# Two attention layers over 2,048 nodes on one core: nine XOR mask tiles instead of six, one compare moved from VectorE to ScalarE, and the part sums placed later

## The chip, the cores and the metric

The kernel runs on one NeuronCore of a Trainium2 chip. It is one program with no partner. The metric is the device time of one execution in microseconds; lower is better. PE is the matmul engine (PEld its weight loads), DVE the vector engine, ACT the scalar engine, POOL and SP the two engines that mostly start transfers.

## The reference

`x` is 2048x512, `adj` 2048x2048 with entries 0 and 1. The program applies a first attention layer (8 heads, over a list of related pairs), a residual, a layer norm, and then the second one, which alone is touched here:

```python
seq = (x @ W_seq).reshape(N, H, DH)                # N = 2048, H = 16 heads, DH = 32
score1 = jnp.einsum('nhd,d->hn', seq, a1)
score2 = jnp.einsum('nhd,d->hn', seq, a2)
scores = score1[:, :, None] + score2[:, None, :]
scores = jax.nn.leaky_relu(scores, negative_slope=ALPHA)
scores = scores + (1.0 - adj)[None, :, :] * MASK_VAL
attn = jax.nn.softmax(scores, axis=-1)
hidden = jnp.einsum('hij,jhd->ihd', attn, seq).reshape(N, D_IN)
```

The kernel forms no matrix of scores. The exponential of a leaky relu of a sum is one of two products of a factor of the target and a factor of the source, and which of them holds depends on the sign of score1 + score2 alone. So for each head it needs a 0/1 mask of neighbours with positive sign ("near") and one of neighbours with negative sign, and multiplies both with values that carry the two source factors.

## The kernel before, in words

The program runs in five blocks with a barrier between them. Block 4 (`stage4`) is the second attention: 16 heads `n`, and in each 16 source tiles `j` of 128 nodes, in an order that is written out in the code and fully unrolled. Each engine runs its own list in order, and semaphores tie the lists.

For one source tile `j` of head `n`:

- A **sign** makes `masks[:, j, :]` (128x2048, fp8) from the sum of scores: on ACT (line 990), or on DVE (`vector_sign`, line 1024) for the tiles in `VECTOR_SIGN`.
- DVE's **mask** (line 1032) ANDs it with the adjacency tile `adjT`.
- For the tiles in `FAR`, DVE's **far** (line 1038) XORs the mask with `nadjT` into `fars`, which is the mask of negative signs. `far(n, j)` stands behind `mask(n, j + 1)`.
- PE's **step** takes the tile in two halves of 1,024 targets, 8 pairs of matmuls in each. A tile in `FAR` costs two matmuls of 99 columns to a pair (lines 1132 and 1133, "far pair"). Any other costs one of 198 columns and one of 99 (lines 1135 and 1136, "near pair"): the negative mask is then the adjacency minus the near mask, by sign and accumulation. Half 1 lags half 0 by `LAG = 4` tiles, so that a head ends with four steps of half 1. `psum_done[0]` and `psum_done[1]` are set by the last step of each half. A head's first step waits for `bank_free[0]`.

Once for each head, among the masks, stand:

- `values(n + 1)` on DVE (lines 1008 and 1012) makes `tmp`, the values of the next head. **part 0** on ACT (line 979) copies it to bf16; `take_off 0` on DVE (line 1019) subtracts that and signals `rest`; **part 1** on ACT copies what is left, and waits for `rest`; `take_off 1` on DVE subtracts again and signals `split`, for which PE's next head waits. Part 0 also waits for `psum_done[1]` of the head before the present one.
- `sum_parts(n - 1, half)` on DVE (line 1047) waits for `psum_done[half]`, adds up the PSUM parts and frees the banks. Then come `scale` (1055), `join` (1063), `invert` (1067) and `norm` (1071).

```python
def part(m, b, p):
    act.wait_ge(*((value, 2 * (m + 1)) if p == 0 else (rest, m + 1)))
    if p == 0 and m >= 2:
        act.wait_ge(psum_done[1], m - 1)
    act.activation(V[:, b, :, p, :], tmp[:, :, :], ACT.Copy).then_inc(hi_out if p == 0 else mid_out, 1)
```

Of the kernel before, what the change touches and what calls it, by code (L numbers as in the profile page):

```python
# [48 lines left out]
HB = 16  # L49
# [879 lines left out]

HALF = N // 2  # L930
HT = HALF // P
VECTOR_SIGN = (3, 8, 13)
FAR = (1, 4, 6, 9, 11, 14)
NS = NT - len(VECTOR_SIGN)
LAG = 4
CZ = 2 * DZ
# [2 lines left out]
def stage4(nc, c, io, t, s, ps):  # L939
# [7 lines left out]
    masks = sb("masks", [P, NT, N], F8)  # L947
    fars = sb("fars", [P, len(FAR), N], F8)
    s1b = [sb(f"s1b{i}", [P, N]) for i in range(2)]
# [11 lines left out]
    with nc.Block() as block:  # L961
        @block.sync
        def _(sp):
            def load(n, b):
                sp.dma_start(s1b[b][:, :], t["s1_rows"][n:n + 1, :].to_broadcast([P, N])).then_inc(s1_in[b], 16)
            load(0, 0)
            load(1, 1)
            for n in range(HB - 2):
                sp.wait_ge(mask_ready, NT * (n + 1))
                load(n + 2, n % 2)  # L970

        @block.scalar
        def _(act):
# [7 lines that stand above are left out]
            def head(n, b):  # L981
                act.wait_ge(s1_in[b], 8 * (n - b) + 16)
                for j in range(NT):
                    if j not in VECTOR_SIGN:

                        if j < NT - 1:
                            act.wait_ge(mask_used, (NT - 1) * n + j + 1)
                        elif n > 0:
                            act.wait_ge(psum_done[1], n)
                        act.activation(masks[:, j, :], s1b[b][:, :], ACT.Relu, bias=t["s2"][:, n, 0, j:j + 1], scale=BIG,  # L990
                                       saturate=False).then_inc(signs, 1)
                    if j in (5, 11) and n < HB - 1:
                        part(n + 1, 1 - b, 0 if j == 5 else 1)
            part(0, 0, 0)
            part(0, 0, 1)
            for n in range(HB):
                head(n, n % 2)

        @block.vector
        def _(dve):  # L1000
# [3 lines left out]
            def values(m):  # L1004

                if m > 0:
                    dve.wait_ge(split, m)
                dve.tensor_tensor(tmp[:, :, :].rearrange("p j (k z) -> p j k z", k=2)[:, :, :, 0:DH],
                                  seq[:, :, None, m * DH:(m + 1) * DH].to_broadcast([P, NT, 2, DH]),
                                  t["e"][:, :, :, m:m + 1].rearrange("p k j o -> p j k o").to_broadcast([P, NT, 2, DH]),  # L1010
                                  ALU.mult).then_inc(value, 1)
                dve.tensor_copy(tmp[:, :, :].rearrange("p j (k z) -> p j k z", k=2)[:, :, :, DH:DZ],
                                t["e"][:, :, :, m:m + 1].rearrange("p k j o -> p j k o")).then_inc(value, 1)

            def take_off(m, b, p):

                dve.wait_ge(hi_out if p == 0 else mid_out, m + 1)
                out = tmp[:, :, :] if p == 0 else V[:, b, :, 2, :]
                dve.tensor_tensor(out, tmp[:, :, :], V[:, b, :, p, :], ALU.subtract).then_inc(rest if p == 0 else split, 1)

            def vector_sign(n, b, j):
                dve.wait_ge(mask_used, (NT - 1) * n + j + 1)
                dve.wait_ge(s1_in[b], 8 * (n - b) + 16)
                dve.tensor_scalar(masks[:, j, :], s1b[b][:, :], t["s2"][:, n, 1, j:j + 1], NEAR, ALU.is_gt, ALU.mult,
                                  saturate=False).then_inc(vector_signs, 1)

            def mask(n, j):
                if j in VECTOR_SIGN:
                    dve.wait_ge(vector_signs, len(VECTOR_SIGN) * n + VECTOR_SIGN.index(j) + 1)
                else:  # L1030
                    dve.wait_ge(signs, NS * n + sum(x not in VECTOR_SIGN for x in range(j)) + 1)
                dve.tensor_tensor(masks[:, j, :].bitcast(U32), masks[:, j, :].bitcast(U32), adjT[:, j, :].bitcast(U32),  # L1032
                                  ALU.bitwise_and).then_inc(mask_ready, 1)

            def far(n, j):

                dve.wait_ge(mask_ready, NT * n + j + 1)
                dve.tensor_tensor(fars[:, FAR.index(j), :].bitcast(U32), nadjT[:, j, :].bitcast(U32),  # L1038
                                  masks[:, j, :].bitcast(U32), ALU.bitwise_xor).then_inc(far_ready, 1)

            def sum_parts(n, half):

                dve.wait_ge(psum_done[half], n + 1)
                if n > 0:
                    dve.wait_ge(scaled, n)
                    dve.wait_ge(joined, n)
                dve.reduce_sum(sums[:, half * HT:(half + 1) * HT, :, :].rearrange("p t k d -> p t (k d)"),
                               ps[:, 4 * half:4 * half + 4, :].rearrange("p b (u c) -> p (b u) c", u=2)[:, :, 0:3 * CZ]
                               .rearrange("p t (s c) -> p t c s", s=3), AX.X).then_inc(summed, 1)
                dve.wait_ge(summed, 2 * n + half + 1)  # L1050
                dve.sem_inc(bank_free[half], 1)

            def scale(n):
                dve.wait_ge(summed, 2 * n + 2)
                dve.tensor_tensor(sums[:, :, :, :], sums[:, :, :, :],
                                  t["w"][:, n, :, :, None].to_broadcast([P, NT, 2, DZ]), ALU.mult).then_inc(scaled, 1)

            def join(n):

                dve.wait_ge(scaled, n + 1)  # L1060
                if n > 0:
                    dve.wait_ge(normed, n)
                dve.tensor_tensor(hid[:, :, :], sums[:, :, 0, :], sums[:, :, 1, :], ALU.subtract).then_inc(joined, 1)

            def invert(n):
                dve.wait_ge(joined, n + 1)
                dve.reciprocal(rz[:, :], hid[:, :, DH]).then_inc(inverse, 1)

            def norm(n):
                dve.wait_ge(inverse, n + 1)  # L1070
                dve.tensor_tensor(seq[:, :, n * DH:(n + 1) * DH], hid[:, :, 0:DH],
                                  rz[:, :, None].to_broadcast([P, NT, DH]), ALU.mult).then_inc(normed, 1)

            def head(n, b):
                for j in range(NT):
                    if j + 1 in VECTOR_SIGN:
                        vector_sign(n, b, j + 1)
                    mask(n, j)
                    if j - 1 in FAR:
                        far(n, j - 1)  # L1080
                    if n > 0:
                        if j == 2:
                            sum_parts(n - 1, 0)
                        if j == 5:
                            sum_parts(n - 1, 1)
                        if j == 7:
                            scale(n - 1)
                        if j == 8:
                            join(n - 1)
                        if j == 9:  # L1090
                            invert(n - 1)
                        if j == 11:
                            norm(n - 1)
                    if n < HB - 1:
                        if j == 1:
                            values(n + 1)
                        if j == 6:
                            take_off(n + 1, 1 - b, 0)
                        if j == 12:
                            take_off(n + 1, 1 - b, 1)  # L1100
            values(0)
            take_off(0, 0, 0)
# [1 line left out]
            for n in range(HB):  # L1104
                head(n, n % 2)
# [9 lines left out]
        def _(pe):  # L1115
            pe.sem_inc(mask_used, NT - 1)

            def step(n, b, half, j):
# [4 lines left out]
                pe.wait_ge(mask_ready, NT * n + j + 1)  # L1123
                if j in FAR:
                    pe.wait_ge(far_ready, len(FAR) * n + FAR.index(j) + 1)
                for i in range(HT):
# [3 lines left out]
                    then = dict(start=False, stop=(j == NT - 1), skip_group_check=True)  # L1130
                    if j in FAR:
                        pe.matmul(out[:, :, 0:DZ], masks[:, j, cols], V[:, b, j, :, 0:DZ], **first)  # L1132
# [215 lines left out]
```

## Time and profile before

| | |
|---|---|
| median of 3 runs | 1426.04 us (1421.89 to 1428.71) |
| profiled execution | 1427.51 us, its span 1426.0 us |
| PE, DVE, ACT, POOL busy over the span | 87%, 75%, 54%, 21% |
| block 4: first sign to last matmul of the last head | 853.14 us to about 1342.5 us |

A row of the timeline gives the start, the length and the engine, line and operation of an instruction, or of several of one kind in a row. The length of one instruction holds a tail in which the next has already begun: what an instruction costs in a full row is the distance from its start to the start of the next.

### The profile page before, as it was taken

How to read it: one execution, taken by the hardware profiler on the slowest of the kernel's cores; microseconds unless marked ns; L12 is line 12 of the kernel's file. 1: busy time of each engine (PE TensorE's matmuls, PEld its weight loads, DVE VectorE, ACT ScalarE, POOL GpSimd, SP SyncE). 2: the span in 40 equal slices, each digit the busy share in tenths (PEclk: the TensorE clock that was granted, in tenths of full speed). 3: DMA queues.
4: the chain of work that ended last, by engine and by line, in shares of the span. 5: the costliest groups of instructions: out<-in, count | busy, mean ns of one | idle time of the engine just before them, and what ended most of it. 6: DMA issues, size and time to landing. Idle time of an engine off the chain costs nothing. (4 is left out here: it accounts for less than half of the span.)

```text
span 1426.0 us, 26813 instructions
## 1 busy us (share of the span) xinstructions
PE 1245.6 (87%) x11026; PEld 839.5 (59%) x11026; DVE 1063.6 (75%) x1411; ACT 764.6 (54%) x763; POOL 306.5 (21%) x247
## 2 busy tenths in 40 slices
PE   4885066999999999989978948999999999999797
PEld 2442022344444444444434528999999999999743
DVE  4576047999999999986214978899898899898455
ACT  2221054454545444442213449899998999989122
POOL 2588643222223233300003630000000000000011
PEclk9998588999999999999998978999999999999999
DMA  6744132122222222212118640000110000100141
GB/s 260 217 116 134 17 70 52 48 68 68 68 68 68 68 48 54 51 27 59 45 41 219 105 105 31 32 31 32 53 40 32 31 32 32 61 32 2 52 148 74
DMA packets 81268, 99.61 MB, mean 70 GB/s; under 512 B 44401, under 2 KB 60032, under 8 KB 79120
## 3 DMA queue, kind: packets, MB, share of 16 engines
q1 hardware_dynamic: 71024, 69.91, 15.6%
q0 software_dynamic: 10144, 28.24, 9.5%
q8 instruction: 78, 1.28, 0.4%
q14 instruction: 22, 0.18, 0.0%
HBM read 88.20 MB, written 20.33 MB: 76 GB/s over the span
## 5 line engine op out<-in xcount | busy, mean ns | idle before, releaser
L990 ACT ACTIVATE s_masks<-s_s1b,s 128x2048 fp8e4<-128x2048 f32 x208 | 396.7, 1987 | 0.0
L1135 PE MATMUL psum<-s_V,s_masks 128*128 128x198 bf16 x2560 | 352.9, 249 | 15.1 <-DVE s_masks L1032 15.1
L1136 PE MATMUL psum<-s_V,nadjT 128*128 128x99 bf16 x2560 | 347.6, 209 | 0.0
L579 ACT ACTIVATE s_exp<-psum,s_negm 128x1536 f32<-128x1536 f32 x96 | 148.0, 1542 | 232.3 <-DVE s_W L648 184.9
L1135 PEld LDWEIGHTS psum<-s_V,s_masks 128*128 128x128 fp8e4 x2560 | 250.2, 98 | 15.7 <-issue 15.4
L1136 PEld LDWEIGHTS psum<-s_V,nadjT 128*128 128x128 fp8e4 x2560 | 250.5, 98 | 0.0
L518 PE MATMUL psum<-h,s_WT 128*128 128x512 f32 x512 | 240.6, 598 | 0.0
L640 DVE TENSOR_SCALAR_CACHE_REDUCE s_junkv<-psum 128x1536 bf16<-128x1536 f32 x96 | 168.5, 1755 | 57.2 <-PE psum L538 55.3
L1032 DVE TENSOR_TENSOR s_masks<-s_masks,adjT 128x512 uint32<-128x512 uint32 x256 | 169.4, 681 | 49.5 <-ACT s_masks L990 47.0
L535 PE MATMUL psum<-f_keys,f_q 128*128 128x512 bf16 x288 | 112.2, 390 | 88.0 <-PEq L221 58.7
L648 DVE SCALAR_TENSOR_TENSOR s_W<-s_exp,s_r,s_W 128x1536 f32<-128x1536 f32 x84 | 179.3, 2135 | 0.2
L1132 PE MATMUL psum<-s_V,s_masks 128*128 128x99 bf16 x1536 | 158.7, 209 | 4.1 <-DVE s_fars L1038 3.4
L1133 PE MATMUL psum<-s_V,s_fars 128*128 128x99 bf16 x1536 | 158.6, 209 | 0.0
L1132 PEld LDWEIGHTS psum<-s_V,s_masks 128*128 128x128 fp8e4 x1536 | 142.3, 98 | 6.1 <-DVE s_masks L1032 3.6
L1133 PEld LDWEIGHTS psum<-s_V,s_fars 128*128 128x128 fp8e4 x1536 | 142.6, 97 | 0.0
L1282 POOL DMA_DIRECT2D out<-s_x x16 | 8.9, 553 | 569.3 <-DVE s_x L1205 569.3
L518 PEld LDWEIGHTS psum<-h,s_WT 128*128 128x128 f32 x512 | 89.5, 192 | 69.7 <-issue 69.7
L535 PEld LDWEIGHTS psum<-f_keys,f_q 128*128 128x128 bf16 x288 | 28.7, 100 | 150.8 <-issue 76.1
L537 PE MATMUL psum<-f_keys,f_q 128*128 128x512 bf16 x288 | 112.2, 390 | 0.0
L536 PE MATMUL psum<-f_keys,f_q 128*128 128x512 bf16 x288 | 112.0, 389 | 0.0
L538 PE MATMUL psum<-f_low,identb 128*128 128x512 bf16 x288 | 111.9, 388 | 0.0
L284 POOL DMA_INDIRECT rel_planes<-s_ones,s_flat x80 | 101.3, 1266 | 49.0 <-issue 33.8
(141 smaller groups left out, 1620.8 us busy)
## 6 DMA issues: line engine op xcount, KB each, us to landing
s_s1b<-s_rows SPq DMA_DIRECT2D x16, 1024.0 KB, 4.7
f_q<-q_parts SPq DMA_DIRECT2D x72, 128.0 KB, 3.2
f_adj<-in_adj POOLq DMA_DIRECT2D x16, 512.0 KB, 5.2
s_adj<-in_adj POOLq DMA_DIRECT2D x16, 512.0 KB, 5.2
rel_planes<-s_zero POOLq DMA_DIRECT2D x3, 2304.0 KB, 19.2
f_rel<-rel_planes SPq DMA_DIRECT2D x36, 192.0 KB, 3.1
f_keys<-s_parts SPq DMA_DIRECT2D x48, 128.0 KB, 2.8
s_x<-x SPq DMA_DIRECT2D x6, 1024.0 KB, 12.3
```

Of the source, the lines that this page charges most:

```text
L518: last = pe.matmul(ps[:, 7, :], WT[m % 2][:, b, :], h[:, 2 * m + b, :], start=(m == 0 and b == 0), stop=(m == HA - 1 and b == 1))
L535: pe.matmul(out, qs[q][:, 0, hd, :], f.k1[:, hd, cols], start=True, stop=False)
L537: pe.matmul(out, qs[q][:, 2, hd, :], f.k2[:, hd, cols], start=False, stop=False)
L579: act.activation(ex[:, hd, :], ps[:, 3 * (hd % 2):3 * (hd % 2) + 3, :].rearrange("p c j -> p (c j)"), ACT.Exp, bias=negm[:, b, hd:hd + 1], ...
L640: dve.tensor_scalar(junkv[:, :], ps[:, 3 * (hd % 2):3 * (hd % 2) + 3, :].rearrange("p c j -> p (c j)"), -1.0, -DIAG, ALU.mult, ALU.min, ac ...
L648: dve.scalar_tensor_tensor(w[:, 0:NE], ex[:, hd, :], r8[:, hd:hd + 1], w[:, 0:NE], ALU.mult, ALU.add).then_inc(added, 1)
L990: act.activation(masks[:, j, :], s1b[b][:, :], ACT.Relu, bias=t["s2"][:, n, 0, j:j + 1], scale=BIG, saturate=False).then_inc(signs, 1)
L1032: dve.tensor_tensor(masks[:, j, :].bitcast(U32), masks[:, j, :].bitcast(U32), adjT[:, j, :].bitcast(U32), ALU.bitwise_and).then_inc(mask_r ...
L1132: pe.matmul(out[:, :, 0:DZ], masks[:, j, cols], V[:, b, j, :, 0:DZ], **first)
L1133: last = pe.matmul(out[:, :, DZ:CZ], fars[:, FAR.index(j), cols], V[:, b, j, :, DZ:CZ], **then)
L1135: pe.matmul(out, masks[:, j, cols], V[:, b, j, :, :], **first)
L1136: last = pe.matmul(out[:, :, DZ:CZ], nadjT[:, j, cols], V[:, b, j, :, DZ:CZ], **then)
```

## The change

Nine tiles instead of six are in `FAR`. `VECTOR_SIGN` has two tiles instead of three, so that ACT makes 14 signs in a head and DVE two. ACT's part 0 stands behind the sign of tile 7 (was 5), part 1 behind that of 12 (was 11). On DVE `values` stands after mask 3 (was 1), the two part sums after masks 4 and 6 (were 2 and 5), `norm` after mask 10 (was 11), `take_off 0` after mask 11 (was 6) and `take_off 1` after mask 14 (was 12).

```diff
-VECTOR_SIGN = (3, 8, 13)
-FAR = (1, 4, 6, 9, 11, 14)
+VECTOR_SIGN = (2, 8)
+FAR = (0, 1, 3, 4, 6, 9, 10, 12, 14)
...
-                    if j in (5, 11) and n < HB - 1:
-                        part(n + 1, 1 - b, 0 if j == 5 else 1)
+                    if j in (7, 12) and n < HB - 1:
+                        part(n + 1, 1 - b, 0 if j == 7 else 1)
...
-                        if j == 2:
+                        if j == 4:
                             sum_parts(n - 1, 0)
-                        if j == 5:
+                        if j == 6:
                             sum_parts(n - 1, 1)
...
-                        if j == 11:
+                        if j == 10:
                             norm(n - 1)
                     if n < HB - 1:
-                        if j == 1:
+                        if j == 3:
                             values(n + 1)
-                        if j == 6:
+                        if j == 11:
                             take_off(n + 1, 1 - b, 0)
-                        if j == 12:
+                        if j == 14:
                             take_off(n + 1, 1 - b, 1)
```

DVE's list before, in head 1, from the second part sum (after mask 5) over `take_off 0` (line 1019, after mask 6) to `join`:

```order
L1047 TENSOR_REDUCE s_sums<-psum 128x528
L1032 TENSOR_TENSOR s_masks<-s_masks,adjT 128x512
L1019 TENSOR_TENSOR s_tmp<-s_tmp,s_V 128x1056
L1024 TENSOR_SCALAR s_masks<-s_s1b,s 128x2048
L1032 TENSOR_TENSOR s_masks<-s_masks,adjT 128x512
L1038 TENSOR_TENSOR s_fars<-nadjT,s_masks 128x512
L1055 TENSOR_TENSOR s_sums<-s_sums,w 128x1056
L1032 TENSOR_TENSOR s_masks<-s_masks,adjT 128x512
L1063 TENSOR_TENSOR s_hid<-s_sums 128x528
```

DVE's list of the change, in head 1, from `invert` (after mask 9) to `take_off 0` (after mask 11) and on to `take_off 1` (after mask 14):

```order
L1067 RECIPROCAL s_rz<-s_hid 128x16
L1032 TENSOR_TENSOR s_masks<-s_masks,adjT 128x512
L1038 TENSOR_TENSOR s_fars<-nadjT,s_masks 128x512
L1071 TENSOR_TENSOR seq<-s_hid,s_rz 128x16x32
L1032 TENSOR_TENSOR s_masks<-s_masks,adjT 128x512
L1038 TENSOR_TENSOR s_fars<-nadjT,s_masks 128x512
L1019 TENSOR_TENSOR s_tmp<-s_tmp,s_V 128x1056
L1032 TENSOR_TENSOR s_masks<-s_masks,adjT 128x512 x2
L1038 TENSOR_TENSOR s_fars<-nadjT,s_masks 128x512
L1032 TENSOR_TENSOR s_masks<-s_masks,adjT 128x512
L1019 TENSOR_TENSOR s_V<-s_tmp,s_V 128x16x66
```

`take_off 0` has moved from before `scale` to behind the whole of `scale`, `join`, `invert` and `norm`, and three masks and two XORs stand between it and `invert`.

ACT's list before, from the first part 0 (line 979) on; the signs between part 0 and part 1 are five, and from part 1 to the next part 0 eight:

```order
L979 ACTIVATE s_V<-s_tmp 128x16x66
L990 ACTIVATE s_masks<-s_s1b,s 128x2048 x5
L979 ACTIVATE s_V<-s_tmp 128x16x66
L990 ACTIVATE s_masks<-s_s1b,s 128x2048 x8
L979 ACTIVATE s_V<-s_tmp 128x16x66
```

The same place of the change:

```order
L979 ACTIVATE s_V<-s_tmp 128x16x66
L990 ACTIVATE s_masks<-s_s1b,s 128x2048 x4
L979 ACTIVATE s_V<-s_tmp 128x16x66
L990 ACTIVATE s_masks<-s_s1b,s 128x2048 x10
L979 ACTIVATE s_V<-s_tmp 128x16x66
```

Four signs now stand between part 0 and part 1 and ten behind part 1; the ten are those of tiles 13, 14 and 15 of the head and of 0, 1, 3, 4, 5, 6 and 7 of the next.

## Rows read from the trace of the kernel before

**Rows 1.** Busy times by window, one head long: PE, PEld, DVE, ACT, POOL, clock, DMA

```profile
core 0: us, PE busy (x) PEld busy (x) DVE busy (x) ACT busy (x) POOL busy (x), PEclk, DMA share, GB/s
930.00:960.00 30.00, 29.96 (x516) 29.83 (x513) 26.85 (x36) 26.66 (x16) 0.00 (x0) 1.00 0.11 37
```

**Rows 2.** Waits from 1005.68 to 1035.68 us: us in total, times, longest

```profile
DVE s_masks L1032 <- ACT s_masks L990: 2.8, 3, 1.3
```

**Rows 3.** Timeline of PE: two near pairs, 31 pairs apart

```profile
1000.19 0.25 PE L1135 MATMUL psum<-s_V,s_masks 128*128 128x198 bf16 x1
...
1004.25 0.25 PE L1135 MATMUL psum<-s_V,s_masks 128*128 128x198 bf16 x1
```

**Rows 4.** Timeline of ACT over one head; in brackets the idle time before

```profile
1012.83 1.09 ACT L979 ACTIVATE s_V<-s_tmp 128x1056 bf16<-128x1056 f32 x1 [3.34 <-PE psum L1136]
...
1023.28 1.07 ACT L979 ACTIVATE s_V<-s_tmp 128x1056 bf16<-128x1056 f32 x1
...
1042.83 1.08 ACT L979 ACTIVATE s_V<-s_tmp 128x1056 bf16<-128x1056 f32 x1 [3.33 <-PE psum L1136]
```

**Rows 5.** Timeline of DVE in the same head

```profile
1004.45 1.22 DVE L1008 TENSOR_TENSOR s_tmp<-seq,e 128x1024 f32<-128x1024 f32 x1
...
1005.68 1.28 DVE L1024 TENSOR_SCALAR s_masks<-s_s1b,s 128x2048 fp8e4<-128x2048 f32 x1
...
1008.15 1.81 DVE L1047 TENSOR_REDUCE s_sums<-psum 128x528 f32<-128x1584 f32 x1
1010.11 1.89 DVE L1032 TENSOR_TENSOR s_masks<-s_masks,adjT 128x512 uint32<-128x512 uint32 x3
...
1016.44 1.25 DVE L1019 TENSOR_TENSOR s_tmp<-s_tmp,s_V 128x1056 f32<-128x1056 f32 x1
1017.61 1.28 DVE L1024 TENSOR_SCALAR s_masks<-s_s1b,s 128x2048 fp8e4<-128x2048 f32 x1
1018.81 0.68 DVE L1032 TENSOR_TENSOR s_masks<-s_masks,adjT 128x512 uint32<-128x512 uint32 x1
1019.41 0.68 DVE L1038 TENSOR_TENSOR s_fars<-nadjT,s_masks 128x512 uint32<-128x512 uint32 x1
1020.01 1.25 DVE L1055 TENSOR_TENSOR s_sums<-s_sums,w 128x1056 f32<-128x1056 f32 x1
1021.18 0.68 DVE L1032 TENSOR_TENSOR s_masks<-s_masks,adjT 128x512 uint32<-128x512 uint32 x1
1021.78 0.70 DVE L1063 TENSOR_TENSOR s_hid<-s_sums 128x528 f32<-128x528 f32 x1
1022.40 0.68 DVE L1032 TENSOR_TENSOR s_masks<-s_masks,adjT 128x512 uint32<-128x512 uint32 x1
1023.00 0.24 DVE L1067 RECIPROCAL s_rz<-s_hid 128x16 f32<-128x16 f32 x1
1023.17 0.62 DVE L1032 TENSOR_TENSOR s_masks<-s_masks,adjT 128x512 uint32<-128x512 uint32 x1
...
1024.91 0.68 DVE L1071 TENSOR_TENSOR seq<-s_hid,s_rz 128x512 f32<-128x512 f32 x1
1025.51 1.28 DVE L1024 TENSOR_SCALAR s_masks<-s_s1b,s 128x2048 fp8e4<-128x2048 f32 x1
```

**Rows 6.** Timeline of ACT at the first signs of the block

```profile
852.15 1.08 ACT L979 ACTIVATE s_V<-s_tmp 128x1056 bf16<-128x1056 f32 x1 [1.32 <-DVE s_tmp L1019]
853.14 9.56 ACT L990 ACTIVATE s_masks<-s_s1b,s 128x2048 fp8e4<-128x2048 f32 x5
```

**Rows 7.** Timeline of DVE: first mask, head 0's second part sum, the last part sum

```profile
855.15 0.69 DVE L1032 TENSOR_TENSOR s_masks<-s_masks,adjT 128x512 uint32<-128x512 uint32 x1 [0.64 <-ACT s_masks L990]
...
892.75 1.81 DVE L1047 TENSOR_REDUCE s_sums<-psum 128x528 f32<-128x1584 f32 x1 [0.16 <-PE psum L1136]
...
1342.55 1.81 DVE L1047 TENSOR_REDUCE s_sums<-psum 128x528 f32<-128x1584 f32 x1 [2.81 <-PE psum L1136]
```

**Rows 8.** Busy times by window around the end of the last head (columns as in rows 1)

```profile
1342.00:1346.00 4.00, 0.51 (x8) 0.32 (x6) 3.27 (x3) 0.00 (x0) 0.00 (x0) 1.00 0.00 0
...
1354.00:1358.00 4.00, 3.92 (x5) 1.83 (x6) 0.00 (x0) 0.00 (x0) 0.00 (x0) 0.51 0.90 246
```

## The prediction, on record before the changed kernel ran

> **What bounds the kernel now.** I looked first at the busy shares of the whole span, where PE leads, and then only at block 4, since no other block is touched. The windows of one head's length show PE busy for 29.96 of 30.00 us, DVE for 26.85, ACT for 26.66 [rows 1]. The reader is to see that PE has no gap, while the two others have about 3 us each. The list of waits of such a head says where these are: DVE waits 2.8 us for signs of ACT [rows 2], and ACT waits 3.34 us for PE, before part 0, which wants the head before to be finished [rows 4]. That is slack: PE holds ACT back. Part 0 begins every 30.00 us (1012.83, 1042.83) [rows 4]. So before, a head costs what its matmuls cost. About 0.5% of this kernel, 7 us, is what its measurement can tell from no change.
>
> **PE's share of the change.** Two near pairs 31 pairs apart start 4.06 us apart, 0.131 us for a pair [rows 3]. A head has 160 near and 96 far pairs; 160 x 0.131 = 20.96, and the 8.99 left of about 29.95 make 0.0936 us for a far pair. Three more far tiles turn 3 x 16 = 48 pairs: 48 x 0.0374 = 1.80 us less. PE then needs 28.15 us a head. If PE still set the pace that would be 16 x 1.80 = 29 us.
>
> **ACT's share.** From part 0 at 1012.83 to part 1 at 1023.28 there are 10.45 us: 0.99 for the part (852.15 to 853.14 [rows 6]), five signs of 1.892 [rows 4]. A head with 14 signs and two parts costs 14 x 1.892 + 1.98 = 28.47 us without a wait, already more than PE's 28.15. So at best the change gives 30.00 - 28.47 = 1.5 us a head.
>
> **DVE's share.** By distance between starts [rows 5]: a mask 0.60 (1021.18 to 1021.78), an XOR 0.60 (1019.41 to 1020.01), a sign 1.20 (1017.61 to 1018.81), `values` 1.23, a part sum with its release of the banks 1.96, `scale` 1.17, `join` 0.62, `invert` 0.17 (the mask behind it is 0.06 shorter than others, 0.62 against 0.68 in length), `norm` 0.60, `take_off` 1.17, or 1.25 until its signal. Three XORs more and a sign less are 1.80 - 1.20 = +0.60. A head's work becomes 9.54 + 5.40 + 2.40 + 1.23 + 3.92 + 1.17 + 0.62 + 0.17 + 0.60 + 2.34 = 27.4 us. No engine alone is over 28.5.
>
> **Where the waits go.** The moved pieces close a loop that was slack before. Part 1 on ACT waits for `take_off 0`. Behind part 1 in ACT's list stand the signs of tiles 13, 14, 15 and of the next head's 0 and 1. DVE's mask 1 waits for that last one, and then goes in order through all up to the next `take_off 0`, for which the next part 1 waits. Before, `take_off 0` stood after mask 6 and part 1 five signs after part 0, so part 1 found it done: no idle time stands before the row at 1023.28 [rows 4]. Now it stands after mask 11 and XOR 10, behind both part sums, `scale`, `join`, `invert` and `norm`. One turn of the loop:
>
> - ACT: part 1 to the first sign 0.99; five signs, the last to its end, 4 x 1.892 + 1.99 = 9.56. Sign to mask is 0.02 to 0.03 (853.14 + 1.99 to 855.15 [rows 6, 7]), and I take the same from `take_off 0` to part 1. Together 10.60.
> - DVE from mask 1: eleven masks 6.54, XORs of tiles 0, 1, 3, 4, 6, 9, 10 4.20, `values` 1.23, two part sums 3.92, the sign of tile 8 1.20, `scale` 1.17, `join` 0.62, `invert` 0.17, `norm` 0.60, `take_off 0` to its signal 1.25. Together 20.90.
>
> The turn is 31.50 us, one head. To enter DVE at a neighbour of mask 1 gives less: at mask 0 it is 1.89 less on ACT and 0.60 + 1.20 more on DVE (31.4), at mask 3 it is 1.89 more and 2.40 less (31.0). So the pace is 31.5: ACT idles 31.5 - 28.5 = 3.0 before part 1, and DVE then starves, since the signs that it wants next are queued behind part 1: with part 1 at time 0, DVE has mask 12 done at 0.5 and waits until sign 13 ends at 3.0; again about 0.7 before masks 14 and 0 each, some 4 us in a head.
>
> I checked what else is late in that clock. XOR 14 ends at 8.0, so PE ends half 0 near 10.6 and the head near 15.25 (0.75, 0.75 and 1.05 for steps 14, 10 and 15; then 1.05, 0.75, 1.05, 0.75, 1.05). DVE reaches the first part sum at 16.0 and the second at 19.8, ACT part 0 at 19.9: none waits for PE. The banks come free at 17.9, so **PE idles some 2.6 us at each head's start**, and 0.7 before step 14. From 17.9 its 28.15 us would end the head at 46.05, 5.2 before the second sum of the next head wants it (51.3).
>
> **The sum.** The first sign starts at 853.14 [rows 6], and nothing ahead of it changes. In head 0 ACT is the pace: part 0 after seven signs at 866.39, four more signs start at 867.38, and tile 11's ends at 873.15; mask 11, XOR 10 and `take_off 0` make it 875.62, part 1 at 875.65. (Head 0's PE end is wanted by the sum at 895.4; before it was there at 892.75 [rows 7], with more matmul work.) Fourteen turns of 31.50 bring the last part 1 to 1316.65. In the last head there is no `values`; mask 4 waits for its sign (14.33), and the banks are free at about 17.45. PE's 28.15 us then end at 1316.65 + 45.6 = 1362.25, against 1342.5 before (the last part sum starts at 1342.55 [rows 7]). That is +19.7 us; block 5 follows as it did. The profiled execution was 1427.51 us, so 1447.2 on its scale; it lay 1.5 above the median of the runs shown, so **1446** for the median. An error of 0.2 us in a turn is 2.8 in the sum; with 0.3 the forecast's own range is 1441 to 1451.
>
> **A rule weighed.** Part 0 idles ACT for 3.34 us [rows 4] though the slot for the sign behind it had been free for some eight half steps of PE: the signs did not pass the waiting part. The Trainium skill, in TensorE: Matmul & The Clock Gate, section Architectural detail, says that the scalar and vector engines have strict first-in first-out queues and that PE alone pulls something ahead, its weight loads. By that rule, with which the trace agrees, part 1 blocks the signs and the turn is 31.5 us; without it ACT would be at 28.5.
>
> **Rivals.**
>
> 1. *ACT alone sets the pace, faster.* The three engines' own sums, 28.15, 28.47 and 27.4, speak for it. If `take_off 0` reached part 1 in time, or a wait of 0.5, a head would take 28.5 to 29.0: 15 heads x 1.0 to 1.5 less gives 1404 to 1411. It decides if DVE's run from mask 1 to the signal is under 28.47 - 10.60 = 17.9 us instead of 20.9. The rows leave no 3 us there. Chance 0.06.
> 2. *About as before.* A turn between 29.5 and 30.4 would do it; it needs 1.1 us or more out of the loop, say starts on DVE closer than 0.60 in a full run. Time 1419 to 1433. Chance 0.05.
> 3. *The clock falls in PE's new gaps, slower still.* PE was idle for about 3.5 us in a window that granted full speed (1342 to 1346), and later ran 3.92 of 4 us at 0.51, the 1.2 GHz level, when it began again after a longer idle time [rows 8]. Such a 4 us costs PE 2 us, and it has 5.2 to spare in a turn, so one dip a head only shows in the last head (+2, 1448). Three or four such stretches cost 6 to 8 us, 0.8 to 2.8 over what is spare; in 14 turns that is 11 to 39 us, 1457 to 1485. The Trainium skill, same page, Part 1: The HAM clock gate, says that idleness brings the clock down to half; by that rule each new gap could cost a dip. The row bears it out only for the longer idle time: 3.5 us of idleness still had full speed, and the new gaps are 2.6. Chance of more than a hidden dip 0.06.
> 4. *The loop as forecast:* chance 0.83, 1441 to 1451.
>
> **How the numbers follow.** Most likely 1446. Range 1438 to 1453: the forecast's own, widened for single waits on semaphores that a full list may show and for the spread of runs (1421.89 to 1428.71). Faster by over 0.5% 0.06, within it 0.05, slower by over 0.5% 0.89.
>
> **What would show it.** Right: ACT's part (line 979) waiting for DVE's `s_tmp` about 3 us, 15 times; DVE's masks waiting for ACT's signs about 4 us a head; PE waiting for the part sum (line 1047) about 2.6 us at each head's start; part 1 coming every 31.5 us; PE busy about 28.2 of 31.5. Wrong: ACT without a gap over two heads (rival 1), PE without one (rival 2), or a granted clock under 1.00 in the middle of block 4 (rival 3).

## The result and the profile after

The changed kernel takes 1448.34 us (median of 6 runs, 1441.08 to 1453.62) against 1424.57 us before (median of 6, 1420.37 to 1428.71). The ratio is 1.0159, with a 95% interval of 1.0122 to 1.0196: slower, and 2.3 us over the forecast of 1446. The profiled execution took 1453.62 us with a span of 1451.7.

The windows of one turn of ACT, 31.60 us long, show where the profile changed (PE, PEld, DVE, ACT, POOL, clock, DMA), against [rows 1]:

```profile
core 0: us, PE busy (x) PEld busy (x) DVE busy (x) ACT busy (x) POOL busy (x), PEclk, DMA share, GB/s
1030.00:1061.60 31.60, 28.39 (x516) 27.93 (x513) 27.56 (x38) 28.55 (x17) 0.00 (x0) 1.00 0.10 35
```

PE, DVE and ACT now each have 3 to 4 us of idle time in a head. None of them is the bound by itself, as the forecast loop between engines has it. The list of waits over thirteen heads (912 to 1322 us; us in total, times, longest) names its links:

```profile
DVE s_masks L1032 <- ACT s_masks L990: 47.3, 39, 2.4
ACT s_V L979 <- DVE s_tmp L1019: 39.5, 13, 3.0
PEld psum L1132 <- issue: 31.8, 19, 2.6
PE psum L1132 <- issue: 28.5, 13, 2.5
```

ACT waits for `take_off 0` 13 times for 3.0 us, and DVE three times a head for ACT's signs, 3.6 us together. PE is idle 13 times before a head's first far pair. No releaser is given there; I take it to be the bank release behind the first part sum, an instruction that the profile does not count as work: one such sum runs from 1021.42 to 1023.22 us and PE starts at 1023.38, and where the wait is shorter the profile names that release (experiment 4). The timeline of ACT shows it in place, where [rows 4] had no idle time before part 1:

```profile
1005.39 1.09 ACT L979 ACTIVATE s_V<-s_tmp 128x1056 bf16<-128x1056 f32 x1 [3.05 <-DVE s_tmp L1019]
1006.38 19.02 ACT L990 ACTIVATE s_masks<-s_s1b,s 128x2048 fp8e4<-128x2048 f32 x10
1025.31 1.07 ACT L979 ACTIVATE s_V<-s_tmp 128x1056 bf16<-128x1056 f32 x1
1026.28 7.67 ACT L990 ACTIVATE s_masks<-s_s1b,s 128x2048 fp8e4<-128x2048 f32 x4
1036.99 1.09 ACT L979 ACTIVATE s_V<-s_tmp 128x1056 bf16<-128x1056 f32 x1 [3.05 <-DVE s_tmp L1019]
```

Part 0 at 1025.31 waits for nothing, where before it waited 3.34 us for PE. DVE's timeline in the same turn:

```profile
1005.27 0.68 DVE L1032 TENSOR_TENSOR s_masks<-s_masks,adjT 128x512 uint32<-128x512 uint32 x1
1008.40 0.69 DVE L1032 TENSOR_TENSOR s_masks<-s_masks,adjT 128x512 uint32<-128x512 uint32 x1 [2.44 <-ACT s_masks L990]
...
1010.29 0.69 DVE L1032 TENSOR_TENSOR s_masks<-s_masks,adjT 128x512 uint32<-128x512 uint32 x1 [0.60 <-ACT s_masks L990]
...
1014.08 0.69 DVE L1032 TENSOR_TENSOR s_masks<-s_masks,adjT 128x512 uint32<-128x512 uint32 x1 [0.60 <-ACT s_masks L990]
1014.68 1.28 DVE L1024 TENSOR_SCALAR s_masks<-s_s1b,s 128x2048 fp8e4<-128x2048 f32 x1
1015.97 0.69 DVE L1032 TENSOR_TENSOR s_masks<-s_masks,adjT 128x512 uint32<-128x512 uint32 x1
...
1025.18 1.80 DVE L1047 TENSOR_REDUCE s_sums<-psum 128x528 f32<-128x1584 f32 x1
1027.20 1.29 DVE L1024 TENSOR_SCALAR s_masks<-s_s1b,s 128x2048 fp8e4<-128x2048 f32 x1 [0.22 <-DVE s_sums L1047]
...
1035.71 1.25 DVE L1019 TENSOR_TENSOR s_tmp<-s_tmp,s_V 128x1056 f32<-128x1056 f32 x1
```

One turn can be read off: part 1 at 1005.39, first sign behind it 1006.38, mask 1 at 1015.97 (10.58 us, forecast 10.60 with the step to part 1), `take_off 0` until 1035.71 + 1.25 = 1036.96 (20.99, forecast 20.90), next part 1 at 1036.99. From mask 1 on DVE has no wait but one of 0.22 behind the second part sum, before it could start tile 8's sign.

The stages ahead of block 4 differ by up to 12 us from one profiled execution to another: the first sign starts at 844 to 856 us in the eleven of this study. So block 4 is also measured by itself, from the first sign to the start of the last part sum. Before, it is 1342.55 - 853.14 = 489.4 us. In the changed kernel, by its timeline:

```profile
856.45 1.99 ACT L990 ACTIVATE s_masks<-s_s1b,s 128x2048 fp8e4<-128x2048 f32 x1
...
1367.05 1.81 DVE L1047 TENSOR_REDUCE s_sums<-psum 128x528 f32<-128x1584 f32 x1 [2.81 <-PE psum L1136]
```

That is 510.6 us, +21.2; the forecast sum was +19.7, and the medians differ by 23.8. The 2.6 us between 21.2 and 23.8 are not in block 4.

### The profile page after: what moved, and what is told of

It is laid out like the page before. It is cut to its first block and busy times, and to the rows that moved or that the text cites. A ratio compares the mean times of both kernels' runs of the same rounds, so it can differ in the third digit from the quotient of the medians.

```text
span 1451.7 us, 26895 instructions
## 1 busy us (share of the span) xinstructions
PE 1225.4 (84%) x10996; PEld 818.3 (56%) x11026; DVE 1072.4 (74%) x1443; ACT 795.0 (55%) x779; POOL 309.6 (21%) x247
## 5 line engine op out<-in xcount | busy, mean ns | idle before, releaser
L990 ACT ACTIVATE s_masks<-s_s1b,s 128x2048 fp8e4<-128x2048 f32 x224 | 427.0, 1987 | 0.0
L1132 PE MATMUL psum<-s_V,s_masks 128*128 128x99 bf16 x2304 | 238.4, 212 | 58.1 <-issue 33.0
L1135 PE MATMUL psum<-s_V,s_masks 128*128 128x198 bf16 x1792 | 259.7, 252 | 0.0
L1136 PE MATMUL psum<-s_V,nadjT 128*128 128x99 bf16 x1792 | 252.8, 210 | 0.0
L1133 PE MATMUL psum<-s_V,s_fars 128*128 128x99 bf16 x2304 | 238.5, 212 | 0.0
L1032 DVE TENSOR_TENSOR s_masks<-s_masks,adjT 128x512 uint32<-128x512 uint32 x256 | 174.8, 683 | 63.2 <-ACT s_masks L990 60.2
L1133 PEld LDWEIGHTS psum<-s_V,s_fars 128*128 128x128 fp8e4 x2304 | 217.1, 99 | 0.0
L1136 PEld LDWEIGHTS psum<-s_V,nadjT 128*128 128x128 fp8e4 x1792 | 177.0, 99 | 0.0
L536 PE MATMUL psum<-f_keys,f_q 128*128 128x512 bf16 x288 | 111.7, 388 | 68.9 <-PEq L221 62.1
L535 PE MATMUL psum<-f_keys,f_q 128*128 128x512 bf16 x260 | 101.3, 390 | 24.1 <-ACT s_exp L579 23.3
L537 PE MATMUL psum<-f_keys,f_q 128*128 128x512 bf16 x286 | 110.7, 387 | 0.0
```

The costliest lines, as they stand in the source:

```text
L535: pe.matmul(out, qs[q][:, 0, hd, :], f.k1[:, hd, cols], start=True, stop=False)
L536: pe.matmul(out, qs[q][:, 1, hd, :], f.k1[:, hd, cols], start=False, stop=False)
L1133: last = pe.matmul(out[:, :, DZ:CZ], fars[:, FAR.index(j), cols], V[:, b, j, :, DZ:CZ], **then)
L1135: pe.matmul(out, masks[:, j, cols], V[:, b, j, :, :], **first)
L1136: last = pe.matmul(out[:, :, DZ:CZ], nadjT[:, j, cols], V[:, b, j, :, DZ:CZ], **then)
```

## The experiments

Theory: the loop through part 1. Rivals tested: the late part sums (PE's new gap at each head's start) and the load of the tables (three more XORs, 14 signs). "Block 4" is the length defined above, of each run's profile; a ratio is to the kernel before on the same chip.

| kernel | ratio (95% interval) | block 4, us |
|---|---|---|
| changed | 1.0159 (1.0122 to 1.0196) | 510.6 |
| 1. `take_off 0` after mask 8 | 0.9801 (0.9758 to 0.9844) | 465.7 |
| 2. kernel before, `take_off 0` after mask 11 | 1.0092 (1.0057 to 1.0127) | 502.4 |
| 3. tables alone | 0.9929 (0.9893 to 0.9966) | 483.2 |
| 4. part sums back to 2 and 5 | 1.0128 (1.0082 to 1.0174) | 508.8 |
| 5. part 1 behind sign 14 | 0.9832 (0.9770 to 0.9893) | 465.8 |
| 6. as 1, part sums back | 0.9867 (0.9811 to 0.9922) | 466.3 |
| 7. `take_off 0` after mask 10 | 1.0035 (1.0005 to 1.0066) | 493.1 |
| 8. tables, both parts and `take_off 0` late | 0.9847 (0.9809 to 0.9884) | 465.7 |
| 9. as 6, part 0 behind sign 5 | 0.9925 (0.9896 to 0.9954) | 476.1 |

### 1. One line moved

```diff
-                        if j == 11:
+                        if j == 8:
                             take_off(n + 1, 1 - b, 0)
```

> The changed kernel with one line moved: take_off 0 stands after mask 8 again ahead of invert and norm, everything else as changed (nine XOR tiles, two DVE signs, part sums after masks 4 and 6). Theory (the loop through part 1): the DVE leg from mask 1 to the signal of take_off 0 loses masks 9, 10, 11, XORs 9 and 10, invert and norm, 21.0 - 3.7 = 17.3 us, so the turn is 10.6 + 17.3 = 27.9 us, under ACT's own 28.5; the idle time of ACT before part 1 goes from 3.0 to near 0 and a head takes 28.5 to 28.8 us. In all 15 x 3.0 = 45 us less than the changed kernel, about 0.984 of the kernel before. Rival (the late part sums, which free the banks late and leave PE a gap of 2.5 us in each head, cause the loss): they stay, so the time stays near 1.016. Rival (more DVE work, three XORs, causes it): stays near 1.016.

Measured: 0.9801, block 4 44.9 us shorter than in the changed kernel. The part sums and the XORs had stayed, so neither rival is enough to cause the loss. ACT's timeline has no idle time left in a turn of 28.46 us:

```profile
1008.47 1.07 ACT L979 ACTIVATE s_V<-s_tmp 128x1056 bf16<-128x1056 f32 x1
1009.45 19.03 ACT L990 ACTIVATE s_masks<-s_s1b,s 128x2048 fp8e4<-128x2048 f32 x10
1028.38 1.07 ACT L979 ACTIVATE s_V<-s_tmp 128x1056 bf16<-128x1056 f32 x1
1029.36 7.67 ACT L990 ACTIVATE s_masks<-s_s1b,s 128x2048 fp8e4<-128x2048 f32 x4
1036.93 1.07 ACT L979 ACTIVATE s_V<-s_tmp 128x1056 bf16<-128x1056 f32 x1
```

A window of one head shows how full all three engines are (columns as above):

```profile
1000.00:1028.46 28.46, 28.15 (x516) 27.93 (x514) 27.46 (x38) 28.46 (x18) 0.00 (x0) 1.00 0.11 39
```

PE 28.15, DVE 27.46, ACT 28.46: the three engine sums of the prediction (28.15, 27.4, 28.47). This version beats the kernel before by 2%, of which block 4, 23.7 us shorter, is 1.7%; there it is bound by ACT alone.

### 2. The suspected line alone, in the kernel before

```diff
-                        if j == 6:
+                        if j == 11:
                             take_off(n + 1, 1 - b, 0)
```

> The kernel before with take_off 0 alone moved from after mask 6 to after mask 11; six XOR tiles, three DVE signs, part sums after masks 2 and 5, part 1 after the sign of tile 11. Theory: the loop closes here too. ACT's leg with entry at mask 2 is 0.99 + 5 x 1.892 + 1.99 = 12.4 us, DVE's from mask 2 to the signal 18.5 us (six of its pieces once, ten masks, four XORs, two signs): a turn of 30.9 to 31.0 us against 30.0, some 13 us slower, 1.009. ACT shows a wait for line 1019 before each part 1. Rivals (part sums, or XORs and signs, cause the loss): no change, 1.000, and no such wait.

Measured: 1.0092, block 4 +13.0 us. The move slows the kernel without a single XOR more and with early part sums. ACT's timeline shows both its waits:

```profile
999.74 1.08 ACT L979 ACTIVATE s_V<-s_tmp 128x1056 bf16<-128x1056 f32 x1 [2.56 <-DVE s_tmp L1019]
1000.73 15.24 ACT L990 ACTIVATE s_masks<-s_s1b,s 128x2048 fp8e4<-128x2048 f32 x8
1017.55 1.09 ACT L979 ACTIVATE s_V<-s_tmp 128x1056 bf16<-128x1056 f32 x1 [1.58 <-PE psum L1136]
1018.55 9.56 ACT L990 ACTIVATE s_masks<-s_s1b,s 128x2048 fp8e4<-128x2048 f32 x5
1030.67 1.09 ACT L979 ACTIVATE s_V<-s_tmp 128x1056 bf16<-128x1056 f32 x1 [2.56 <-DVE s_tmp L1019]
```

DVE's timeline shows where the loop enters its list, and where it leaves it:

```profile
1010.33 0.69 DVE L1032 TENSOR_TENSOR s_masks<-s_masks,adjT 128x512 uint32<-128x512 uint32 x1 [1.20 <-ACT s_masks L990]
...
1029.38 1.25 DVE L1019 TENSOR_TENSOR s_tmp<-s_tmp,s_V 128x1056 f32<-128x1056 f32 x1
```

The turn is 30.93 us, expected 30.9 to 31.0, but the sum in the expectation was put together wrongly and came out right by luck. It entered DVE at mask 2 and counted the sign of tile 3, which stands ahead of mask 2. The entry is at mask 1, at 1010.33: ACT's leg is 10.59 us from part 1, DVE's 20.30 until `take_off 0` ends at 1030.63, and 0.04 lead to part 1. The wait for PE before part 0 is still there at 1.58 us, but it costs nothing: the loop leaves ACT's list at the sign of tile 1, ahead of part 0, and so does not pass through that wait.

### 3. The tables alone

```diff
-VECTOR_SIGN = (3, 8, 13)
-FAR = (1, 4, 6, 9, 11, 14)
+VECTOR_SIGN = (2, 8)
+FAR = (0, 1, 3, 4, 6, 9, 10, 12, 14)
```

> Of the change only the two tables: nine XOR tiles and two DVE signs; all pieces that stand once in a head stay where they were. Theory: no loop, ACT's 28.47 us sets the pace, 28.5 to 28.9 us a head, 18 to 24 us faster than before, 0.984 to 0.988. Rival (the load of the XORs on DVE or the 14 signs on ACT cause the loss): near 1.016. Rival (with DVE fuller, masks come late to PE): between 1.00 and 1.01.

Measured: 0.9929. Neither my 0.984 to 0.988 nor either rival: faster than before, but block 4 gained 6.2 us of the 23.7 that experiment 1 shows to be there. ACT still waits for PE before part 0, 0.5 and 1.9 us in turns, so that two heads take 59.53 us (980.93 to 1040.46):

```profile
980.93 1.08 ACT L979 ACTIVATE s_V<-s_tmp 128x1056 bf16<-128x1056 f32 x1 [1.91 <-PE psum L1136]
...
1009.99 1.09 ACT L979 ACTIVATE s_V<-s_tmp 128x1056 bf16<-128x1056 f32 x1 [0.49 <-PE psum L1136]
...
1040.46 1.08 ACT L979 ACTIVATE s_V<-s_tmp 128x1056 bf16<-128x1056 f32 x1 [1.91 <-PE psum L1136]
```

And PE waits for an XOR of DVE, up to 1.73 us:

```profile
1018.82 0.21 PE L1132 MATMUL psum<-s_V,s_masks 128*128 128x99 bf16 x1 [1.73 <-DVE s_fars L1038]
```

Each holds up the other, in a second loop, which takes two heads for a turn. More rows of ACT and of DVE show its links:

```profile
992.37 17.13 ACT L990 ACTIVATE s_masks<-s_s1b,s 128x2048 fp8e4<-128x2048 f32 x9
...
1003.85 0.69 DVE L1032 TENSOR_TENSOR s_masks<-s_masks,adjT 128x512 uint32<-128x512 uint32 x1
...
1017.99 0.68 DVE L1038 TENSOR_TENSOR s_fars<-nadjT,s_masks 128x512 uint32<-128x512 uint32 x1
```

Part 0 at 980.93 holds back the signs behind it, and the sixth of the nine from 992.37 on, tile 1's, ends as mask 1 starts at 1003.85: 22.92 us. DVE has no idle time from there to the XOR of tile 6 (1017.99), and PE starts that tile at 1018.82: 14.97. PE then has no gap up to the end of its head, for which part 0 at 1040.46 waits: 21.64. Together that is 59.53 us, where ACT's own work for two heads is 56.9. Experiments 6, 8 and 9 look for what opens this loop.

### 4. The part sums back

```diff
-                        if j == 4:
+                        if j == 2:
                             sum_parts(n - 1, 0)
-                        if j == 6:
+                        if j == 5:
                             sum_parts(n - 1, 1)
```

> The changed kernel with the two part sums back after masks 2 and 5. Theory: both still lie between mask 1 and take_off 0, so the turn stays at 31.5 to 31.6 us and the time at 1.016; PE's gap at each head's start shrinks or moves, and nothing is gained by it. Rival (the late sums cause the loss): the time falls to 0.984 to 1.00.

Measured: 1.0128, block 4 508.8 us against 510.6. ACT's wait stays at 2.98 us and its turn is 31.54 (1000.41 to 1031.95). The 0.06 a turn is the wait behind the second part sum, which a mask follows here. PE's idle time did not shrink, it moved (912 to 1290 us, twelve heads):

```profile
PE psum L1132 <- DVE s_fars L1038: 21.6, 48, 0.8
PE psum L1132 <- DVEq L1051: 9.6, 12, 0.8
```

A head starts 0.8 us late, by the bank release that is named here (line 1051), and the rest is in four short waits for XORs. So the long gap at the head's start was no cost of its own.

### 5. Part 1 behind sign 14

```diff
-                    if j in (7, 12) and n < HB - 1:
+                    if j in (7, 14) and n < HB - 1:
```

> The changed kernel with one number changed on ACT: part 1 stands behind the sign of tile 14 (changed kernel: 12); take_off 0 stays after mask 11 on DVE. Theory: the turn now has three signs behind part 1 (15, 0, 1) in place of five, 31.6 - 3.8 = 27.8 us, under ACT's 28.5, so ACT's idle time goes and a head takes 28.5 to 28.9 us: 0.980 to 0.985 of the kernel before. Should it be the place of take_off 0 on DVE alone that matters (the length of DVE's list ahead of it delays PE's masks), the time stays near 1.016.

Measured: 0.9832, block 4 465.8 us, no wait before either part. DVE's list is that of the changed kernel, instruction for instruction, `take_off 0` after mask 11 included. So its late place costs nothing in itself; only together with the signs queued behind part 1 does it close the loop.

### 6. Experiment 1 with early part sums

The edits of experiments 1 and 4 together.

> The changed kernel with take_off 0 after mask 8 and with the part sums back after masks 2 and 5. Tells what the late part sums are worth once the loop is open. Theory: the second sum has to wait for PE's end of a head, and XOR 6, for which PE waits, then stands behind it, so a head takes 28.9 to 29.5 us, 0.988 to 0.993 as with the tables alone. Rival (the later part 0, behind sign 7, is what the version with the tables alone lacked): 28.5 us a head, 0.980.

Measured: 0.9867, its interval overlaps that of experiment 1 (0.9801), and block 4 is 466.3 against 465.7 us. ACT runs without a gap. My theory for experiment 3, that the early second sum holds PE's masks up, falls: with early sums the loss is nil here. What experiment 3 lacked is among the other places: `values`, the two parts, `take_off 0` and `take_off 1`, `norm`. The difference of the two medians (1395.43 and 1406.31 us) does not come from block 4; in the profiled executions the first sign starts at 844.42 and 855.27 us. The granted clock from 150 to 300 us, far ahead of block 4, was 0.86 in the first and 0.81 in the second.

### 7. A dose

```diff
-                        if j == 11:
+                        if j == 10:
                             take_off(n + 1, 1 - b, 0)
```

> The changed kernel with take_off 0 after mask 10 (it was 11 in the changed kernel and 8 in an earlier run). A dose: DVE's leg loses mask 11 and XOR 10, 1.2 us, so the theory gives a turn of 31.60 - 1.20 = 30.40 us and 1.8 us of idle time before part 1; 15 x 1.2 = 18 us less than the changed kernel, 1.003 of the kernel before. If the loss were a threshold or had another cause, it would be 1.016 or 0.980.

Measured: 1.0035, as expected; ACT's timeline:

```profile
999.11 1.08 ACT L979 ACTIVATE s_V<-s_tmp 128x1056 bf16<-128x1056 f32 x1 [1.84 <-DVE s_tmp L1019]
...
1029.52 1.08 ACT L979 ACTIVATE s_V<-s_tmp 128x1056 bf16<-128x1056 f32 x1 [1.84 <-DVE s_tmp L1019]
```

The turn is 30.41 us (expected 30.40): one mask and one XOR less in DVE's leg, 1.2 us, are 1.19 us less a head. What stands in the leg comes through in full.

### 8 and 9. What the tables alone lacked

Experiment 8 takes the tables alone and moves the copies:

```diff
-                    if j in (5, 11) and n < HB - 1:
-                        part(n + 1, 1 - b, 0 if j == 5 else 1)
+                    if j in (7, 12) and n < HB - 1:
+                        part(n + 1, 1 - b, 0 if j == 7 else 1)
...
-                        if j == 6:
+                        if j == 8:
                             take_off(n + 1, 1 - b, 0)
```

> The version with the tables alone (0.993), with the copies moved besides: part 0 behind sign 7, part 1 behind sign 12, take_off 0 after mask 8. The part sums stay after masks 2 and 5, values after mask 1, norm after 11, take_off 1 after 12. With the tables alone ACT waited for PE before part 0, 0.5 and 1.9 us in turns, and PE for XORs. If part 0 stood too early there, ACT now runs without a gap and a head takes 28.5 us: block 4 from first sign to last part sum 466 us in place of 483, 0.982 to 0.987. If it was the early part sums or values, it stays at 483 us, 0.993.

Measured: 0.9847, block 4 465.7 us, no wait before a part. So `values`, `norm`, `take_off 1` and the sums could have stayed; the place of the two copies and of `take_off 0` was what experiment 3 lacked. Experiment 9 takes number 6 and moves part 0 alone back:

```diff
-                    if j in (7, 12) and n < HB - 1:
-                        part(n + 1, 1 - b, 0 if j == 7 else 1)
+                    if j in (5, 12) and n < HB - 1:
+                        part(n + 1, 1 - b, 0 if j == 5 else 1)
```

> The version with take_off 0 after mask 8 and the part sums after masks 2 and 5 (466 us for block 4), with one number changed: part 0 behind the sign of tile 5 in place of 7. If part 0 behind sign 5 makes ACT wait for PE's end of a head, the wait of 0.5 to 1.9 us before part 0 comes back and block 4 takes 475 to 485 us, 0.990 to 0.995. If the place of part 0 does not matter, it stays at 466 us.

Measured: 0.9925 and 476.1 us, in the range expected, but by another wait than I had named: not for PE, but for `values`:

```profile
1002.23 1.09 ACT L979 ACTIVATE s_V<-s_tmp 128x1056 bf16<-128x1056 f32 x1 [0.68 <-DVE s_tmp L1012]
...
1031.48 1.09 ACT L979 ACTIVATE s_V<-s_tmp 128x1056 bf16<-128x1056 f32 x1 [0.70 <-DVE s_tmp L1012]
```

DVE, in between:

```profile
1025.14 0.69 DVE L1032 TENSOR_TENSOR s_masks<-s_masks,adjT 128x512 uint32<-128x512 uint32 x1
...
1027.56 1.80 DVE L1047 TENSOR_REDUCE s_sums<-psum 128x528 f32<-128x1584 f32 x1
1029.51 0.69 DVE L1032 TENSOR_TENSOR s_masks<-s_masks,adjT 128x512 uint32<-128x512 uint32 x1
```

This is a third loop, of one head: from part 0 at 1002.23 over ACT's signs to mask 1 at 1025.14, then on DVE without idle time through the first part sum and `values` to part 0 at 1031.48, 29.25 us in all. The part sum makes up 1.95 of them. Without it 27.3 would be left, under ACT's 28.5, so by this estimate it takes the late `values` and the early sum together; that was not run.

A part 0 that stands early makes ACT wait, for whichever of its two conditions is late: PE's end of the head before where `values` stands after mask 1 (experiment 3), `values` where it stands after mask 3 and behind the first part sum (here). Whether part 0 alone, without part 1 and `take_off 0`, would have cured experiment 3 was not tried. An estimate says yes: two signs less between part 0 and sign 1 are 2 x 1.892 = 3.8 us less in its loop, 55.7 for two heads, under ACT's 56.9.

## Why the prediction was right, point by point

**The bound.** Right. The kernel before was PE's, and the three engine sums of the changed kernel were met to 0.1 us in experiment 1, where no loop disturbs them.

**The loop.** Right, and shown from three sides: with `take_off 0` earlier (1, 7), with fewer signs behind part 1 (5), and in the kernel before with only that line moved (2). The turn was 31.60 for a forecast 31.50. The 0.10 lies on DVE's leg, 20.99 in place of 20.90: 0.06 is the step from the second part sum to the sign of tile 8 (2.02 us, 1025.18 to 1027.20), which I priced like the step to a mask (1.96 [rows 5]). 14 turns of 0.10 are 1.4 of the 1.5 us by which block 4 passed the forecast; I had the mechanism and mis-sized this one term. Of the signs that I had listed, ACT's wait of 3.0 us came 14 times and not 15, since in head 0 it is 0.63, and DVE's waits are 3.6 us in a head in place of 4.

**The walk to the loop's first and last turn.** Part 1 of head 0 comes 22.53 us after the first sign (856.45 to 878.98, forecast 853.14 to 875.65, 22.51), and the last part sum starts 45.6 us after the last part 1 (1321.41 to 1367.05, forecast 45.6).

**The median.** Block 4 is where the sum was put to the test: 510.6 us against 489.4 + 19.7 = 509.1. That the median came within 2.3 us of 1446 is in part luck. The six runs spread over 12.5 us, the first sign of the profiled execution came 3.3 us later than before (856.45 against 853.14), and the sum had nothing for that.

**PE's gap at each head's start.** Right in kind: 28.5 us over 13 heads, 2.2 each against 2.6. The mean hides two sizes. In the twelve heads that start from 960 to 1308 us the gap is 2.47 us six times and 1.94 six times. It is 1.94 in a head that follows one with a fall of the clock (below), in which PE's work took longer. In the others PE also waits some 0.7 us, but for the XOR of tile 12 (1041.44, 4.45 us after part 1), where I had placed this wait before step 14. The gap's price of nothing was right (experiment 4).

**The rule weighed.** Its conclusion stands, and one reading in it was low: when ACT began to wait for PE, the slot for the sign behind part 0 had been free for about ten half steps (an estimate from their lengths), and not eight.

**The rival of ACT alone.** It did not occur, but its price was about right. 1404 to 1411 was given for the case that the signal came in time. The four versions in which it did (experiments 1, 5, 6 and 8) measured 1395.43, 1400.41, 1406.31 and 1404.85 us, and their block 4 was 23.1 to 23.7 us shorter than before, where the rival had at most 15 x 1.5 = 22.5. What the first two have beyond that is not from block 4.

**The rival of the clock.** The step that was wrong in its evidence, and in the sign given for it. I argued that 3.5 us of idleness before had left the granted clock at 1.00 [rows 8], and so 2.6 would. That window holds only the first part of a longer stretch. PE went on being idle, for 5.54 us in all, and the clock fell before it started again:

```profile
1346.00:1347.00 1.00, 0.00 (x0) 0.00 (x0) 0.93 (x3) 0.00 (x0) 0.00 (x0) 1.00 0.00 0
1347.00:1348.00 1.00, 0.00 (x0) 0.00 (x0) 0.52 (x1) 0.00 (x0) 0.00 (x0) 0.83 0.00 0
1348.00:1349.00 1.00, 0.95 (x5) 0.98 (x6) 0.00 (x0) 0.00 (x0) 0.00 (x0) 0.50 0.00 0
```

So [rows 8] could not show what a short gap followed by work would do. The windows around a gap of the changed kernel (columns as above) show a fall from a shorter one:

```profile
1112.00:1116.00 4.00, 4.00 (x74) 4.00 (x72) 4.00 (x8) 4.00 (x3) 0.00 (x0) 1.00 0.02 6
1116.00:1120.00 4.00, 2.06 (x30) 1.90 (x29) 3.85 (x6) 4.00 (x3) 0.00 (x0) 0.82 0.02 4
1120.00:1124.00 4.00, 4.00 (x63) 3.91 (x62) 3.78 (x5) 4.00 (x4) 0.00 (x0) 0.75 0.00 0
```

PE was idle for 1.94 us, ran again at full speed for a moment, and then at half: its timeline has starts 0.045 us apart until 1118.55, and 0.09 apart from 1118.68. By the list under "What would show it", a clock under 1.00 in the middle of block 4 was to mean rival 3; it was there, and the time was still the loop's. What I had worked out for such a dip did hold. One dip a head hides in the 5.2 us that PE has to spare in a turn: ACT's waits, 3.03 to 3.05 us, are the same in heads with a dip and without one. The Trainium skill, in TensorE: Matmul & The Clock Gate, section Part 1: The HAM clock gate, says that idleness takes the clock from 2.4 to 1.2 GHz; the trace agrees that it can happen around gaps of 1.94 us (0.82 and 0.75 in the windows above), and here it cost no time.

## What to carry to other kernels

Sum up loops, not engines. Three engines at 28.2, 28.5 and 27.5 us made a turn of 31.6 because an in-order wait on one engine stood between a late piece of another and the work that this other wanted next. For each wait that a change moves, list what is queued behind it, go from there to the engine that wants it, and on to the signal waited for: that sum is a lower bound of the period, whatever the busy shares say.

The cure is then cheap. Move the waited-for piece ahead in its list, or the wait back in its own: either one took out the whole 3 us (experiments 1 and 5), while undoing the late part sums, which looked costly, shortened block 4 by 1.8 us of the 44.9 (experiment 4).

## What the runs showed of the hardware that was not expected

The granted clock fell after an idle stretch of 1.94 us (above), while in the kernel before it was still 1.00 from 1346 to 1347 us, with PE idle since 1342.5. It fell in some heads of the changed kernel and not in others, whatever the gap's length: behind the gaps of 2.47 us it fell three times of six, and behind those of 1.94 us three times of six. In fourteen windows of 31 or 32 us from 880 to 1323 us the granted clock was 0.94 or 0.95 in seven and 1.00 in seven; two of them:

```profile
1133.00:1165.00 32.00, 30.06 (x556) 29.89 (x553) 27.56 (x37) 28.95 (x17) 0.00 (x0) 1.00 0.10 35
...
1228.00:1260.00 32.00, 30.06 (x522) 29.82 (x521) 27.56 (x37) 28.96 (x17) 0.00 (x0) 0.95 0.10 35
```

DVE and ACT are as busy in the one as in the other. So an idle time that one gap survives is no proof for the next.
